# A decoder block on one core: its prologue with value products taken per input chunk, their weights made first, the context turned into four banks, and another order of loads

## The reference

```python
x = layernorm(x + attn(x))            # layer 1
x = layernorm(x + cross_attn(x, ctx)) # layer 2
x = layernorm(x + moe_ffn(x))         # 16 experts, 4 of them per token
```

```python
attn  = softmax(q @ k.T * SCALE + ENT * (eq @ ek.T) * SCALE * decay)
a     = sigmoid(x @ amp_w.T + amp_b)
p     = tanh(x @ ph_w.T + ph_b) * pi
sup   = einsum('bhsd,hod->bhso', v, mix_w) + mix_b
mixed = v + SUP*a*cos(p)*sup + SUP*a*sin(p)*roll(sup, 1, axis=-1)
ctx   = attn @ mixed
y     = layernorm(x + ctx @ Wo.T + bo) * ln_g + ln_b
```

## Time and profile before

| | us |
|---|---|
| median of 3 runs | 419.49 |
| lowest, highest | 419.38, 422.47 |
| the profiled execution | 421.96 |
| its span in the trace | 420.0 |
| PE busy | 363.9 (87%) |
| DVE busy | 277.1 (66%) |
| ACT busy | 227.5 (54%) |
| POOL busy | 217.1 (52%) |

### The profile page before, as it was taken

The page is one execution under the profiler, slowest core; times in us unless marked ns, Lnnn a source line. Parts: engine busy times, 40 slices in busy tenths (PEclk is TensorE's granted clock), DMA queues, the critical chain, the costliest instruction groups (busy, mean ns, idle before and its releaser), DMA issues. The chain is left out here.

```text
span 420.0 us, 11906 instructions
## 1 busy us (share of the span) xinstructions
PE 363.9 (87%) x3620; PEld 261.0 (62%) x3620; DVE 277.1 (66%) x1296; ACT 227.5 (54%) x495; POOL 217.1 (52%) x403
## 2 busy tenths in 40 slices
PE   2695878899989999888598999999888989999992
PEld 1673656667666677666476777777663745566661
DVE  6553978888888889886354767767763245644443
ACT  1426467678877877657548667676353242222220
POOL 8639244677766776567475332331113335355542
PEclk9977599999999999999779999999999989999998
DMA  6877676656666666532424334333004520163300
GB/s 130 232 141 140 155 123 129 124 112 130 130 129 120 126 134 123 89 47 57 107 66 108 90 92 109 92 83 95 2 2 150 181 75 2 35 198 108 118 25 25
DMA packets 50427, 43.40 MB, mean 103 GB/s; under 512 B 21776, under 2 KB 43104, under 8 KB 48848
## 3 DMA queue, kind: packets, MB, share of 16 engines
q1 hardware_dynamic: 49344, 42.29, 44.1%
q0 software_dynamic: 512, 0.48, 0.9%
q10 hardware_dynamic: 528, 0.10, 0.1%
HBM read 32.24 MB, written 10.62 MB: 102 GB/s over the span
## 5 line engine op out<-in xcount | busy, mean ns | idle before, releaser
L1452 DVE CUSTOM_DVE_ANT_0 bank<-bank,decayed_e 128x128 f32<-128x128 f32 x256 | 66.8, 322 | 1.0
L635 POOL TENSOR_TENSOR stk<-stk 128x512 f32<-128x512 f32 x32 | 40.6, 1269 | 45.8 <-ACT stk L1309 43.7
L1463 DVE TENSOR_REDUCE top<-bank 128x4 bf16<-128x512 f32 x64 | 44.2, 691 | 30.2 <-PE bank L721 30.0
L1102 ACT ACTIVATE prob<-bank 128x512 f32<-128x512 f32 x64 | 38.2, 597 | 32.4 <-PE bank L700 31.8
L1700 DVE TENSOR_TENSOR stk<-bank,stk 128x512 f32<-128x512 f32 x32 | 22.1, 691 | 50.5 <-POOL stk L635 50.4
L1441 DVE TENSOR_TENSOR decayed_e<-bank,decay 128x512 f32<-128x512 f32 x64 | 43.9, 686 | 16.9 <-issue 16.5
L1309 ACT ACTIVATE stk<-bank 128x512 f32<-128x512 f32 x32 | 19.0, 597 | 60.3 <-PE bank L1013 60.3
L471 POOL TENSOR_TENSOR rest<-pf,parts 128x512 f32<-128x512 f32 (+1 forms) x32 | 29.2, 914 | 40.2 <-ACT parts L1091 40.2
L1026 PEld LDWEIGHTS bank<-w,stk 128*128 128x128 f32 x256 | 33.4, 192 | 22.0 <-DVE stk L1700 14.5
L477 POOL TENSOR_TENSOR parts<-rest,parts 128x512 bf16<-128x512 f32 (+1 forms) x32 | 29.3, 915 | 26.7 <-ACT parts L1095 26.7
L768 PE MATMUL bank<-prob_t,vmix 128*16 128x128 f32 x768 | 39.4, 278 | 0.1
(11 more groups left out here) (204 smaller groups left out, 829.5 us busy)
## 6 DMA issues: line engine op xcount, KB each, us to landing
stk<-parts_dram SPq DMA_DIRECT2D x128, 64.0 KB
stk<-shares_dram SPq DMA_DIRECT2D x64, 128.0 KB, 3.0
parts_dram<-parts SPq DMA_DIRECT2D x16, 384.0 KB, 5.4
stk<-parts_dram SPq DMA_DIRECT2D x112, 32.0 KB
stk<-parts_dram SPq DMA_DIRECT2D x16, 192.0 KB
parts_dram<-parts SPq DMA_DIRECT2D x16, 192.0 KB, 2.4
stk<-parts_dram SPq DMA_DIRECT2D x16, 128.0 KB
w<-in_L_ffn_w_dram SPq DMA_DIRECT2D x3, 512.0 KB, 13.0
```

Of the source, the lines that this page charges most:

```text
L635: pool.tensor_tensor(h1[kk % 2], sg[kk % 2], share[kk], ALU.mult).then_inc(weighted, 1)
L1102: act.activation(prob[g % 2][:].rearrange("p h t -> p (h t)"), bank[g % 2][:], ACT.Exp).then_inc(L.exped, 1)
L1452: m = dve.tensor_tensor_reduce(out=bank[g % 2][:, 128 * j:128 * j + 128], in0=bank[g % 2][:, 128 * j:128 * j + 128], in1=decayed_e[:, g % ...
L1463: dve.tensor_reduce(top[:, b.par, GH * g:GH * g + GH], bank[0][:].rearrange("p (h t) -> p h t", h=GH), AX.X, ALU.max).then_inc(L2.maxed, 1)
```

## The change

It touches the prologue and the first slot of layer 1, and no arithmetic.

- POOL clears `stk[1]` ahead of its DMA issues, not behind them, and the seven bias rows are loaded by ACT's queue, ahead of ACT's six loads.
- Each later chunk of x has a semaphore of its own.
- PE turns `mix_bd_n` ahead of the other weights, and DVE copies `mix_bd` first; `entangled(Batch(0, 1))` stands behind the last step of `wall` and `row_bias`; `neg_ident` and `ident_bf` are made after the last value product.
- PE turns x chunk by chunk (1, 2, 3) and makes four value products behind each; ACT's `take_x` and `middle` calls are reordered to fit.
- The context chunks go to banks 4, 5, 7 and 6, so that their turning does not wait for ACT's copies.
- Banks 4 and 5 are cleared by DVE in the first slot of layer 1, behind the mixing factors. PE's waits for `act_set` 8 and for that clearing stand at the second and fourth unit of that slot. ACT no longer waits for `DV_END`.
- POOL runs `xl_all` behind `slot1(0, 1)`, not ahead of it. DVE's wait for `pool_set` 2 stays where it was.

```diff
@@ semaphores and counts @@
-        in_x = sem("in_x")
+        in_x = [sem(f"in_x{c}") for c in range(1, NCH)]
...
-        PE_QK, PE_BIAS, PE_W, PE_MIX, PE_SUP, PE_VSZ, PE_C = 1, 2, 5, 6, 10, 10, 26
+        PE_QK, PE_BIAS, PE_MIX, PE_W, PE_SUP, PE_C = 1, 2, 4, 6, 7, 26
+        PE_VSZ = [8 + b + min(b // 4, 2) for b in range(NB)]
-        DV_BIAS, DV_QK, DV_COLS, DV_MIX, DV_SUP, DV_WALL = 2, 6, 10, 11, 23, 27
+        DV_BIAS, DV_QK, DV_COLS, DV_MIX, DV_SUP, DV_WALL = 2, 6, 10, 11, 14, 25
-        X_BANK, C_BANK = (4, 5, 7, 4), (5, 7, 4, 5)
+        X_BANK, C_BANK = (4, 5, 7, 4), (4, 5, 7, 6)
@@ POOL @@
-            for r, n in enumerate(("L0_attn_bq", ... "L0_attn_bv")):
-                pool.dma_start(bias_rows[r:r + 1, :], a[n].unsqueeze(0)).then_inc(in_bias, 16)
+            pool.memset(stk[1][:]..., 0.0).then_inc(zeroed[1], 1)
             rows(row_in[:, 0:D], a["L0_attn_bv"])
...
             rows(bo2[:], a["L0_xattn_bo"])
-            pool.memset(stk[1][:]..., 0.0).then_inc(zeroed[1], 1)
...
             slot1(0, 0)
             pool.wait_ge(in_rows, 9 * 16)
             pool.tensor_tensor(xb_all[:], x_tok[:], ...).then_inc(pool_set, 1)
+            slot1(0, 1)
             pool.tensor_tensor(xl_all[:], x_tok[:], ...).then_inc(pool_set, 1)
-            slot1(0, 1)
@@ PE @@
             project(L1, Batch(0, 0), True)
+            pe.transpose(bank[3][:, 0:128], mix_bd_n..., ident[:]).then_inc(pe_set, 1)
             ...
             project(L1, Batch(0, 1), True)
-            pe.transpose(bank[3][:, 0:128], mix_bd_n..., ident[:]).then_inc(pe_set, 1)
-            pe.wait_ge(in_x, 3 * 16)
-            for c in range(1, 4):
-                turn_x(c)
             pe.wait_ge(dve_set, DV_SUP)
             pe.matmul(bank[0][:, 0:128], wn[:, WV, :], mix_bd[:], start=True, stop=True)
             pe.matmul(bank[0][:, 128:256], bv_cols[:], mix_bd[:], ...).then_inc(pe_set, 1)
+            def first_values(lo, hi):
+                for b in range(lo, hi):
+                    pe.wait_ge(dve_set, DV_WALL + max(b - 3, 0))
+                    pe.wait_ge(act_set, b // 4 + 1)
+                    pe.matmul(bank[b % 4][:, 0:VSZ], x_t[:, 128 * b:128 * b + 128], wall[:],
+                              start=True, stop=True).then_inc(pe_set, 1)
+            pe.wait_ge(in_x[0], 16)
+            turn_x(1)
+            first_values(0, 4)
+            pe.wait_ge(in_x[1], 16)
+            turn_x(2)
             project(L1, Batch(1, 0), True)
+            first_values(4, 8)
+            pe.wait_ge(in_x[2], 16)
+            turn_x(3)
+            first_values(8, 12)
+            project(L1, Batch(1, 1), True)
+            first_values(12, NB)
-            pe.wait_ge(dve_set, DV_WALL)
-            pe.wait_ge(act_set, 4)
-            for b in range(NB):
-                ... the 16 value products, project(L1, Batch(1, 1), True) behind b == 7
             pe.wait_ge(in_c, 4 * 16)
+            pe.wait_ge(act_set, 4)
             for c in range(4):
-                pe.wait_ge(act_set, c + 2)
+                if c == 3:
+                    pe.wait_ge(L1.proj_ev, 8)
+                    pe.wait_ge(L1.ent_ev, 8)
                 ... turn c_tok chunk c into bank[C_BANK[c]]
             pe.wait_ge(dve_set, DV_END)
-            pe.wait_ge(act_set, 8)
...
-            slot1(0, 1)
+            for g in range(NG):
+                if g == 1:
+                    pe.wait_ge(act_set, 8)
+                if g == 3:
+                    pe.wait_ge(dve_set, DV_END + 2)
+                unit1(Batch(0, 1), g)
@@ ACT @@
+            for r, n in enumerate(("L0_attn_bq", ... "L0_attn_bv")):
+                act.dma_start(bias_rows[r:r + 1, :], a[n].unsqueeze(0)).then_inc(in_bias, 16)
...
-            for par in range(2):
-                take_projection(L1, Batch(0, par), True)
-                high(L1, Batch(0, par), True)
-                take_x(1 + par)
-                middle(L1, Batch(0, par))
-            take_x(3)
+            take_projection(L1, Batch(0, 0), True)
+            high(L1, Batch(0, 0), True)
+            middle(L1, Batch(0, 0))
+            take_projection(L1, Batch(0, 1), True)
+            high(L1, Batch(0, 1), True)
+            take_x(1)
+            take_x(2)
+            middle(L1, Batch(0, 1))
             take_projection(L1, Batch(1, 0), True)
             high(L1, Batch(1, 0), True)
+            take_x(3)
             slot1(0, 0)
...
-            act.wait_ge(dve_set, DV_END)
@@ DVE, in slot1(0, 1) @@
                     mixing_factors()
+                    dve.wait_ge(act_set, 8)
+                    for half in range(2):
+                        step(dve.memset(bank[4 + half][:], 0.0))
```

More of the change, by code:

```diff
@@ L865, in _ @@
             project(L1, Batch(0, 0), True)
+            pe.wait_ge(in_small, 5 * 16)
+            pe.wait_ge(dve_set, DV_MIX)
+            pe.transpose(bank[3][:, 0:128], mix_bd_n[:].rearrange("p h f -> p (h f)"), ident[:]).then_inc(pe_set, 1)
             pe.wait_ge(in_w, 6 * 16)
-            pe.wait_ge(in_small, 5 * 16)
             for i, w in enumerate((WV, WO, XQ, XK)):
@@ L1383, in _ @@
             entangled(Batch(0, 0))
-            dve.wait_ge(in_const, 16)
-            step(dve.tensor_scalar(neg_ident[:], ident[:], -1.0, None, ALU.mult))
-            step(dve.tensor_copy(ident_bf[:], ident[:]))
+            dve.wait_ge(pe_set, PE_MIX)
+            n = step(dve.tensor_copy(mix_bd[:], bank[3][:, 0:128]))
+            assert n == DV_SUP
             dve.wait_ge(pe_set, PE_W - 1)
@@ L1396, in _ @@
             step(dve.tensor_copy(gate_t[:], bank[2][:, 288:304]))
-            dve.wait_ge(pe_set, PE_MIX)
-            n = step(dve.tensor_copy(mix_bd[:], bank[3][:, 0:128]))
-            assert n == DV_SUP
-            entangled(Batch(0, 1))
             dve.wait_ge(in_rows, 9 * 16)
@@ L1407, in _ @@
             assert n == DV_WALL
-            entangled(Batch(1, 0))
+            entangled(Batch(0, 1))
             after(n)
             for b in range(NB):
-                dve.wait_ge(pe_set, PE_VSZ + b + 1)
+                dve.wait_ge(pe_set, PE_VSZ[b] + 1)
                 n = step(dve.tensor_tensor(vsz[:, b, :], bank[b % 4][:, 0:VSZ], row_bias[:], ALU.add))
-                if b == 8:
+                if b == 3:
+                    entangled(Batch(1, 0))
+                if b == 11:
                     entangled(Batch(1, 1))
-            dve.wait_ge(act_set, 8)
-            for p in range(2):
-                n = step(dve.memset(bank[4 + p][:], 0.0))
+            dve.wait_ge(in_const, 16)
+            step(dve.tensor_scalar(neg_ident[:], ident[:], -1.0, None, ALU.mult))
+            n = step(dve.tensor_copy(ident_bf[:], ident[:]))
             assert n == DV_END
```

23 lines of the change are left out of this document (8 added, 15 removed).

## The result

| us | before | changed |
|---|---|---|
| median beside each other | 420.27 (4 runs) | 426.28 (4 runs) |
| lowest, highest | 419.38, 422.47 | 424.83, 427.81 |
| the profiled execution, its span | 421.96, 420.0 | 425.14, 423.3 |

The changed kernel takes 1.0138 times as long, with a 95% interval of 1.0098 to 1.0178. I had forecast 421.0, with 424.0 as the upper end. The direction was right (slower), the size was not: +1.5 us was forecast, and +6.0 measured between the medians. Between the two profiled executions the spans differ by 3.3. The ratios leave out executions that ran in a slower state or stood far off, such as one of 1124.02 in e9 and one of 1819.41 of the kernel before.

The account below looks back on a forecast made before the run. PE and DVE were taken as nearly full in layer 1, a fixed train, so only its start could move. Pick wait 1.2 plus clock 1.6 minus saved load wait 1.3 gave +1.5 on 419.5: 421.0, range 416.5 to 424.0.

Parts of the forecast that it names:

- `wall`, values, issue of stack load 0: Prologue: `wall` ready at about 17.6, stack load 0 issued at 23.0, last `vsz` at about 30 in place of 33.4.
- First score: Batch 0's start: PE waits for stack load 0, landing 11.7 behind its issue, so 34.7, 5.7 ahead of before.
- Batch 0, the clearing, the remainder, the sum: Layer 1's first slot: second `pick` at 40.9 including 1.0 of clearing, POOL's remainder at 47.6, `xl_all` from 48.7, taking 4.52.
- The wait that comes in its place: Ahead of batch 1: DVE waits for `pool_set` 2 until 53.2, so batch 1's first `pick` comes 1.2 us later than before.
- The clock: Start of batch 1: PE at clock 0.50 for one and a half units, costing 1.6 us, bounds 0 and 4.6.
- The baseline: Whole kernel: median taken 2.5 below the profiled execution's 421.96, so 419.5 plus 1.5 gives 421.0.
- rival 3: Prologue: clock falls while PE waits for `wall`, moving stack load 0 and all behind it by 2.4: 423.4; chance 0.14.
- Rival 1: Ahead of batch 0: stack load 0 lands early, at 31 to 33, whole 2 to 4 us earlier; chance 0.12.
- Rival 2: Ahead of batch 1: the wait for `pool_set` costs nothing because `xl_all` runs early: 414.8; chance 0.06.
- my three signs of being wrong: Layer 1: `xl_all` starting before 45, first score before 33, or the later rhythm not keeping the shift.
- The step held beside POOL: Prologue: `neg_ident` on DVE held beside `xb_all` until 34.4, first score about 34.9, sum +1.7 in place of +1.5.

Follow-up runs that it names:

- e9: The changed kernel with DVE waiting for `pool_set` 1, `xl_all` in four parts behind four POOL slots, banks cleared before the first score: 417.3, 0.993 of before.
- e8: The changed kernel measured again without an edit, for a second trace: 425.6, 1.014 of before.
- e10: The kernel of e9 plus 12 extra turns on PE while it waits for `wall`: 415.8, 0.9922 of before.
- e2: The changed kernel with POOL's order kept, but DVE waiting for `pool_set` 1 instead of 2: 419.23, 0.9977 of before.
- e5: The kernel of e1 with stack load 0 ahead of spill 1 in SP's queue: 425.21, 1.0107 of before.
- e7: The kernel of e5 with `neg_ident` and `ident_bf` made before the row loads land and the bank clearing given to ACT: 423.73, 1.0095 of before.
- e0: The kernel before, measured again without an edit, for a second trace: 419.8 (416.84 to 426.39), trace span 415.4.
- e1: The changed kernel with `xl_all` moved back ahead of POOL's first slot: 419.62, 0.998 of before.
- e3: The kernel before with one move alone, `xl_all` behind POOL's slot of batch 0: 427.95, 1.0197 of before.
- e6: The changed kernel plus 36 extra turns on PE between batch 0 and batch 1, while DVE waits for the sum: 424.04, 1.0114 of before.
- e4: The kernel of e1 plus 36 extra turns on PE ahead of the first score: 421.58, 1.0006 of before.

## Why the prediction missed

**`wall`, values, issue of stack load 0: right.** 17.2 for 17.6, 22.70 for 23.0, last `vsz` 28.7 for 30, the context copies at 34.1 for 35.5.

**First score: right in kind, short in size.** PE waits for stack load 0, as forecast, but it lands 13.1 us behind its issue (12.2 in e8), where I put 11.7 from two indirect reckonings. That is a first score at 35.8 and 37.0 in place of 34.7. Why it takes longer stays open. The loads with a spill just ahead of them took 12.0 (e10) to 13.3 (e2), those of e5 and e7, with none just ahead, 11.6 and 12.1; and stack load 2, on which I leant, took 11.7 in the first trace of before and 10.75 in e0.

**Batch 0, the clearing, the remainder, the sum: right.** First score to second `pick` 6.30 for 6.2; from there to ACT's cast 6.07 for 5.95 plus the 0.7 to POOL as forecast; `xl_all` 1.1 behind the remainder's start, and 4.49 long. Of the 1.3 by which batch 1's first `pick` is later than forecast (54.54 for 53.25), 1.1 is the first score's.

**The wait that comes in its place: right, and it is the whole loss.** e1, e2 and e3 show it from three sides: undone in the changed kernel it gives back 6.7, with only the wait changed 7.1, and done alone in the kernel before it costs 7.3, each as much as the 5.4 to 6.0 by which the changed kernel is slower, or more. DVE idled for 6.23 us, but the trace did not name POOL as the releaser, as I had said it would.

**The clock: right in kind, 2.2 for 1.6** (e6, by its trace).

**The baseline: this is the step that failed.** I wrote that the median lies 2.5 below the profiled execution's 421.96 and took the same 2.5 off the changed kernel. The arithmetic of the miss is short. The steps gave 423.5 for a profiled execution, the first one was 425.14: 1.6 too little, of which 1.1 is the landing of stack load 0 and most of the rest the clock. That execution then lay 1.1 under its median of 426.28, where I had taken 2.5 off: another 3.6. Together these make 5.3, the distance from 421.0 to 426.28. (The median of before itself came to 420.27, 0.8 above the 419.49 that I had, so that the loss was sized 4.5 too small.) The profiled execution of before was one in which the first eight value products ran at half clock (0.76 over the stretch) and the clock came back late in batch 0, which put its batch 2 at 61.67; e0 reached it at 58.98. I set steps at full clock against a baseline at half clock, and so booked as small a loss that is 5 to 6 us by the medians, and 5.0 at batch 2 by the mean of two traces each. I even had this clock as rival 3, but only as something that could befall the changed kernel; it befalls both, in some executions (first trace of before, e1, e8) and not in others (e0, e2, the first trace of the changed kernel). That a single trace can lie to either side of its median is shown; what makes an execution the one kind or the other, and the 1.9 us behind batch 2 in e0, stay open.

**The rivals.** Rival 1 did not come: the earliest landing of stack load 0 is the 32.6 of e5, where it was issued 1.7 earlier. Rival 2 is what e2 makes true, and it gives 419.2, not the 414.8 that I wrote for it. The gain of the prologue is spent on the way. Held against e0, e2's first score is 3.0 earlier (36.28 for 39.26), its first `pick` of batch 1 only 0.3, and its batch 2 begins at 59.08 for 58.98: 1.1 went on the clearing, 1.6 on the stretch at half clock, and the rest in batch 1, where PE waited 1.07 for mixed values. Why the clock came back sooner in e0, which starts batch 0 later, no run here isolates; in e4 PE did not idle ahead of the first score, and the clock was at 0.50 from 45 to 50 us all the same. Rival 3's mechanism occurred, in e8: stack load 0 out 2.1 later (24.76 for 22.70), but the first score and batch 2 only 1.1 later, not the 2.4 that I wrote. A loss of over 1% had a chance of 0.10. None of my three signs of being wrong showed, since all three concern the steps, and the step that failed lies behind them.

**The step held beside POOL.** A DVE step was held beside `xb_all`, though not the one that I named: `neg_ident`, at 28.60, lasted 0.65 us, and `ident_bf` behind it 4.54. The two lasted 0.21 and 0.22 in e5, where POOL was idle. For this I had cited SBUF — State Buffer, § Who interferes with whom, of the Trainium skill; the trace agrees with it. The rows:

```profile
28.77 0.21 DVE L1434 TENSOR_SCALAR neg_ident<-ident 128x128 bf16<-128x128 f32 x1
28.90 0.22 DVE L1435 CAST ident_bf<-ident 128x128 bf16<-128x128 f32 x1
```

In the earlier trace rows the held step is recorded 0.25 us ahead of POOL's clearing, so those rows show that it is held, and not that the later one is. The hold cost nothing in the changed kernel, since it was over at 33.7 and stack load 0 landed at 35.8. The 0.2 us that I priced for it was not there.

## What to carry over

When a large, unhurried piece of work is moved behind a slot, look for the waits that count past it on other engines: here one number in DVE's wait (2 where 1 was enough) turned a harmless move into 7 us, and giving the wait its true count, cutting the sum into parts and clearing in idle time made the kernel 0.7% faster than before (e9). Price a change against an execution whose clock and waits are those the changed kernel will have, and if the times of one kernel scatter by more than the effect, take a second trace before trusting a difference of marks. When a load is put ahead of a store in a queue, ask who waits for the store.

## What the runs showed of the hardware

- The same kernel, with the same instructions, ran its first value products at 1.2 or at 2.4 GHz from one execution to the next: eight value matmuls took 3.90 us in e8 and 2.21 in the first trace of the changed kernel, PE having waited 2.02 and 0.80 for `wall`. The wait alone does not decide it: in e9 PE had waited 2.81 us and they took 2.21. I had not expected nine of ten times of one kernel (e0) to spread from 416.84 to 421.76, as much as the effect that was to be found.
- A `tensor_tensor` of DVE whose two inputs are in SBUF is held as well: 4.73 us in place of 0.42 in e5, beside `xl_all`. SBUF — State Buffer, § Who interferes with whom, of the Trainium skill says that a DVE instruction with two SBUF inputs contends with a GpSimd instruction that reads SBUF, and this trace agrees. A `pick`, with one of its inputs in PSUM, took its usual 0.69 beside the same sum in e2 (at 51.51, within 50.49 to 55.04). What is held shows as its own duration, not as idle time before it.
- Extra turns on PE kept the clock at 1.00 where PE would have stood idle (e6, and e4 until 37 us). They shortened what followed only in e6, by 2.2 us; in e4 the clock had a mean of 0.50 again from 45 to 50 us.
